# A vision tower on one core: from whole pairs over two drain turns to halves of a pair, one half-step apart

## The reference, cut to what matters

```python
q_feat = bilinear_sample(feature_map, ref)                    # 32 x 32 grid
h = gelu(layer_norm(q_feat @ W_o1 + b_o1, ln_g, ln_b))
sampled = bilinear_sample(feature_map, ref + off(h) * scale)  # 8 points for each token
out = softmax(q . k) @ v                                      # over the 8 points
...
h = concatenate([cls_tok, out])                               # 1025 tokens
x = layernorm(h); y = wkv(decay, first, x1 @ Wk, x1 @ Wv)     # recurrence over tokens
x = x + (sigmoid(x1 @ Wr) * y) @ Wo
x = x + sigmoid(h2 @ Wr_ffn) * (square(relu(h2 @ Wk_ffn)) @ Wv_ffn)
h = h + x;  h = h + relu(expert[argmax(router)](layernorm(h)))
```

## Time and profile before

| | |
|---|---|
| median of 3 runs | 2804.71 us (2804.19 to 2809.35) |
| profiled execution, its own time | 2803.6 us |
| its span (first to last instruction) | 2801.7 us |
| busy: PE, DVE, ACT, POOL | 2391.6, 2385.7, 1350.2, 1983.2 us |
| mean granted TensorE clock | 0.952 of full speed |
| transfers | 314.70 MB, of which 268.57 MB gathers |

### The profile page before, as it was taken

One profiled execution on the slowest core, in us unless ns is written; L12 is line 12 of the kernel. 1 busy time (PEld: TensorE's weight loads), 2 busy tenths in 40 slices (PEclk: granted clock), 3 DMA queues, 4 the chain that ended last, 5 costly groups with the idle time before them and its releaser, 6 DMA issues. The chain is left out here.

```text
span 2801.7 us, 34581 instructions
## 1 busy us (share of the span) xinstructions
PE 2391.6 (85%) x10646; PEld 1561.1 (56%) x10680; DVE 2385.7 (85%) x3808; ACT 1350.2 (48%) x2326; POOL 1983.2 (71%) x2052
## 2 busy tenths in 40 slices
PE   4588889888988888898888889888888988889887
PEld 4455555655655555655555556555556556555533
DVE  5889989889998989998898989888998988888741
ACT  2345444544544444464444446444444645444563
POOL 4777777777777777777777777777777777777400
PEclk7799999999999999999999999999999999999999
DMA  4333333434343343434334343433434343333200
GB/s 161 118 119 117 119 119 103 126 118 127 118 126 118 105 123 116 127 117 127 118 111 128 108 126 118 125 118 113 127 106 126 118 125 119 111 104 103 72 0 15
DMA packets 139228, 314.70 MB, mean 112 GB/s; under 512 B 68912, under 2 KB 69296, under 8 KB 134960
## 3 DMA queue, kind: packets, MB, share of 16 engines
q0 software_dynamic: 98304, 268.57, 32.7%
q1 hardware_dynamic: 40880, 45.58, 4.8%
HBM read 305.62 MB, written 8.40 MB: 112 GB/s over the span
## 5 line engine op out<-in xcount | busy, mean ns | idle before, releaser
L471 POOL DMA_INDIRECT gathered<-pixels,index x2048 | 1983.0, 968 | 649.2 <-issue 614.8
L527 PE MATMUL points_ps<-c_sb,weighed 128*128 128x128 f32 x4096 | 542.4, 290 | 230.8 <-DVE weighed L1063 230.3
L1063 DVE TENSOR_TENSOR weighed<-gathered,tables 128x1024 f32<-128x1024 f32 x512 | 600.4, 1214 | 125.8 <-DMA gathered<-pixels,index 123.9
L527 PEld LDWEIGHTS points_ps<-c_sb,weighed 128*128 128x128 f32 x4096 | 494.9, 150 | 339.7 <-DVE weighed L1063 286.4
L539 PE MATMUL kv_ps<-kv_sb,sampled_t 128*128 128x256 f32 x2048 | 473.4, 385 | 26.6 <-DVE products L1091 26.4
L721 ACT ACTIVATE sampled_t<-points_ps 128x512 f32<-128x512 f32 x256 | 153.1, 598 | 710.1 <-PE points_ps L527 710.1
L539 PEld LDWEIGHTS kv_ps<-kv_sb,sampled_t 128*128 128x128 f32 x2048 | 388.0, 192 | 112.6 <-DVE products L1091 41.2
L617 PE MATMUL work_ps<-nm,w_sb 128*128 128x512 f32 x544 | 291.6, 619 | 38.0 <-DVE xm L1253 35.3
L486 PE MATMUL work_ps<-hn,w_sb 128*128 128x512 f32 x544 | 267.4, 616 | 12.9 <-DVE hn L1115 10.2
L849 ACT ACTIVATE moe_hidden<-work_ps,v_sb 128x512 f32<-128x512 f32 x272 | 186.7, 687 | 161.5 <-PE work_ps L618 144.2
L1098 DVE TENSOR_REDUCE scores<-products 128x128 f32<-128x1024 f32 x128 | 246.0, 1922 | 0.0
(11 more groups left out here) (169 smaller groups left out, 3124.4 us busy)
## 6 DMA issues: line engine op xcount, KB each, us to landing
grid_px<-grid SPq DMA_DIRECT2D x32, 1024.0 KB, 5.6
gathered<-pixels,index POOLq DMA_INDIRECT x2048, 2.7
out<-rm SPq DMA_DIRECT2D x32, 256.0 KB
w_sb<-weights SPq DMA_DIRECT2D x1, 1984.0 KB, 8.9
moe_hidden<-consts SPq DMA_DIRECT2D x1, 512.0 KB, 9.8
attended<-cls SPq DMA_DIRECT2D x1, 512.0 KB, 11.5
c_sb<-consts SPq DMA_DIRECT2D x1, 192.0 KB, 5.2
w_sb<-weights SPq DMA_DIRECT2D x1, 192.0 KB, 5.1
```

Of the source, the lines that this page charges most:

```text
L471: pool.indirect_dma_start(gathered[:, n % RING, k * PATCH:(k + 1) * PATCH], None, pixels, bass.IndirectOffsetOnAxis(ap=index[:, n // TILES ...
L527: mm = pe.matmul(points_ps[:, j * P:(j + 1) * P], weighed[:, n % 2, at:at + 2 * C], ident, is_transpose=True, start=(q == 0), stop=(q == 3))
L1063: ins = dve.tensor_tensor(to[:, :, :, e, :], g[:, :, e, :, :], wt[:, :, e, :].unsqueeze(3).broadcast_to([P, HEADS // 2, 4, C]), ALU.mult)
```

## The change

The pipeline's unit becomes half a pair: 512 tokens of both images. A turn still samples one pair in 32 slots, but in its first 16 slots it samples the first half of both images and in its last 16 the second half. The mix and the experts run on halves, in parts: A is the first part of the mix ("early": `in` to `wo` and `add_mix`) on half 0 of the pair being sampled, in slots 20 to 31 of the same turn; B is the rest ("late": `cenf` to `dn`) of that half, in slots 0 to 4 of the next turn; C is both for half 1 (early in slots 4 to 15, late in 16 to 20); D and E are the experts for halves 0 and 1 (slots 5 to 15 and 21 to 31). One template of 16 slots is used for both half-steps, and the `LAST_` tables are gone. One turn without sampling follows turn 15 (turn 16: B, C, D and E). Turn 0 has only C and E for the class token, in half 1, and A.

Every stage that waited for two halves, and every ACT or DVE operation on 1024 tokens, becomes one on 512 that is done twice. The grid's load and the output's store, which SP issues, are split in the same way: each half-step loads 512 KB from each of two images and stores 128 KB to each of two. On SP the order in a turn was load, load, store; it is load, store, load, store, and a store waits for ACT's copy of `out` (slot 15 of its half-step).

```diff
-PIECES = 4
-PIECE = NQ // PIECES
+PIECES = 2
+PIECE = HALF // PIECES
...
-SCHEDULE = [
-    (0, 1, ["in0"]), (1, 2, ["cenm0", "cenm1"]), (2, 1, ["cena0"]), (2, 2, ["varm0", "varm1"]), (2, 1, ["vara0"]),
...
+TEMPLATE = [
+    (0, "late", ["cenf"]), (0, "late", ["varf"]), (1, "late", ["gate"]), (1, "late", ["up.0", "up.1"]),
+    (2, "late", ["up.2", "up.3"]), (3, "late", ["dn"]), (4, "query", ["qt0", "qt1"]), (4, "early", ["in"]),
...
+PART_OF = {"late": "BC", "early": "AC", "expert": "DE", "query": ("q0", "q1")}
+PART_SLOT = {"late": (0, 16), "early": (16, 0), "expert": (0, 16), "query": (0, 16)}
...
+EARLY_AT = {"mix_input": 6, "running_max": 8, "running_sums": 10, "mixed_sums": 12, "mixed_exponent": 13, "mixed": 14,
+            "add_mix": 15}
+LATE_AT = {"ffn_input": 1, "gate_exponent": 2, "add_ffn": 4}
+EXPERT_AT = {"moe_input": 6, "take_logits": 8, "choose": 9, "add_moe": 14}
...
             def iteration(it):
                 parts = parts_of(it)
-                for b in range(2):
+                for h in range(2):
                     if "q0" in parts:
-                        load_grid(it, b)
-                if 2 in parts:
-                    store(it)
+                        load_grid(it, h)
+                    if "DE"[h] in parts:
+                        store(it, "DE"[h])
...
-            def ffn_input(it):
-                for h in range(2):
-                    dve.wait_ge(stds_f.sem, stds_f.at(it, h + 1))
-                    dve.tensor_tensor(hn[:, cols(h)], xc[:, cols(h)], rs1[:, cols(h)],
-                                      ALU.mult).then_inc(ffn_in_ready.sem, 1)
...
+            def ffn_input(it, part):
+                run, h = run_of(it, part), half_of(part)
+                dve.wait_ge(stds_f.sem, stds_f.at(run, h))
+                dve.tensor_tensor(hn[:, cols(h)], xc[:, cols(h)], rs1[:, cols(h)], ALU.mult).then_inc(ffn_in_ready.sem, 1)
```

More of the change, by code:

```diff
@@ L57 @@
 T_GRID = 4 * TILES * HEADS
-T_DECAY = T_GRID + 4 * TILES
+T_DECAY = T_GRID + 2 * 4 * TILES
 SLOTS = 4 * (2 * TILES) // 2
-SCHEDULE = [
[11 rows of a table removed]
-]
[L80 to L86, removed]
@@ new lines, with schedule @@
+PART_OF = {"late": "BC", "early": "AC", "expert": "DE", "query": ("q0", "q1")}
+PART_SLOT = {"late": (0, 16), "early": (16, 0), "expert": (0, 16), "query": (0, 16)}
+def schedule():
+    rows = []
+    for half in range(2):
+        for slot, stage, names in TEMPLATE:
+            h = 1 - half if stage == "early" else half
+            rows.append((16 * half + slot, PART_OF[stage][h], names))
+    return rows
+SCHEDULE = schedule()
+QUERY_AT = {"grid_corners": 2, "features": 7, "normalised": 11, "gelu": 13, "sampling_points": 15}
@@ L97, with work_uses @@
 QUERIES_AT = (17, 1)
-LAST_SCHEDULE = [
[8 rows of a table removed]
[L108 to L116, removed]
 ROUND = float(2 ** 23)
 GELU_CUBE = 0.044715
-def work_uses(schedule, parts):
-    names = [(part, name) for _, part, group in schedule if part in parts for name in group]
+def work_uses(parts):
+    names = [(part, name) for _, part, group in SCHEDULE if part in parts for name in group]
     return {key: n for n, key in enumerate(names)}, len(names)
@@ L393, in all_iterations @@
                     steps.restart(eng)
-            for it in range(last_looped + 1, pairs + 2):
+            for it in range(last_looped + 1, pairs + 1):
                 turn(it)
@@ L415, in load_grid @@
                 sp.sem_inc(grid_requested.sem, 1)
[L416 to L433 removed]
+                of = slice(b * TILES // 2 * PATCH, (b + 1) * TILES // 2 * PATCH)
@@ new lines, in gate, with expert @@
+            def gate(run, h):
+                act.wait_ge(gate_exp_arg.sem, gate_exp_arg.at(run, h))
+                act.activation(rs2[:, cols(h)], rs2[:, cols(h)], ACT.Exp, scale=-1.0).then_inc(gate_ready.sem, 1)
+            def expert(it, part, names):
+                run, h, name = run_of(it, part), half_of(part), names[0]
+                if name == "cenm":
+                    act.wait_ge(written[h].sem, written[h].at(run - 1 + h, 0))
+                    centered(it, part, "cenm", xm, rm)
+                if name == "varm":
+                    inverse_stds(it, part, "varm", rm, stds_m.sem)
+                if name == "one":
+                    bank, done = full(act, it, part, "one")
+                    act.activation(choice_t[:, cols(h)], bank, ACT.Copy)
+                    act.activation(others_t[:, cols(h)], bank, ACT.Identity, bias=minus1_col).then_inc(done, 1)
+                if name.startswith("mu"):
+                    for use in names:
+                        k = int(use[-1])
+                        bank, done = full(act, it, part, use)
+                        at = V_MB1 + k % BLOCKS
+                        act.activation(moe_hidden[:, k, :], bank, ACT.Relu,
+                                       bias=v_sb[:, at:at + 1]).then_inc(done, 1)
+                if name == "out":
+                    bank, done = full(act, it, part, "out")
+                    act.activation(rm[:, cols(h)], bank, ACT.Copy).then_inc(done, 1)
@@ L1203, in gate_exponent, with add_mix @@
-            def gate_exponent(it):
-                dve.wait_ge(gate_log.sem, gate_log.at(it, 2))
-                for c in range(PIECES):
-                    last = dve.tensor_tensor(rs2[:, piece(c)], rs2[:, piece(c)], relu_r[:, piece(c)], ALU.add)
+                        step(dve.tensor_copy(state[:, 0:1], state[:, HALF + 1:HALF + 2]))
+            def add_mix(it, part):
+                h = half_of(part)
+                bank, done = full(dve, it, part, "wo")
+                dve.tensor_tensor(x1[:, cols(h)], x1[:, cols(h)], bank, ALU.add).then_inc(done, 1)
@@ L1305, in iteration @@
-                    if 2 in parts:
-                        if j == vector_at["moe_input"]:
-                            moe_input(it)
-                        if j == vector_at["take_logits"]:
-                            take_logits(it)
-                        if j == vector_at["choose"]:
-                            choose(it)
-                        for h in range(2):
-                            if j == vector_at[f"add_moe{h}"]:
-                                add_moe(it, h)
+                    for name, stage in (("ffn_input", ffn_input), ("gate_exponent", gate_exponent), ("add_ffn", add_ffn)):
+                        for part in parts_at(it, j, "late", LATE_AT[name]):
+                            stage(it, part)
@@ new lines, in iteration @@
+                    for name, stage in (("mix_input", mix_input), ("running_max", running_max),
+                                        ("running_sums", running_sums), ("mixed_sums", mixed_sums),
+                                        ("mixed_exponent", mixed_exponent), ("mixed", mixed), ("add_mix", add_mix)):
+                        for part in parts_at(it, j, "early", EARLY_AT[name]):
+                            stage(it, part)
+                    for name, stage in (("moe_input", moe_input), ("take_logits", take_logits), ("choose", choose),
+                                        ("add_moe", add_moe)):
+                        for part in parts_at(it, j, "expert", EXPERT_AT[name]):
+                            stage(it, part)
```

726 lines of the change are left out of this document (355 added, 371 removed), and 18 rows, old and new, of tables (LAST_SCHEDULE, SCHEDULE).

## The result

The changed kernel takes 3320.7 us (median of 4 runs, 3317.83 to 3322.5), the kernel before 2804.45 beside it: a ratio of 1.1836, interval 1.1815 to 1.1856. Forecast was 3341, with 3229 to 3477 for the likeliest case. The profiled run has a span of 3319.7 us and a mean granted clock of 0.903.

A forecast was written before the change was run, and what follows sets the result against it. POOL was taken to set the pace at 81.5 us a half-step, DVE next at 74.7. First half-step 120, 31 half-steps of 100.6 making 3118.6, drain 100.2: span 3338.8, so 3341 us, range 2980 to 3480.

The forecast's parts named there:

- the likeliest case: Whole kernel: half-steps of 97 to 105 us, 3229 to 3477 us in all, given 52%.
- What bounds the kernel: Sampling turns: POOL sets the pace at 81.5 us per half pair; DVE is occupied for 74.7, leaving 6.8 us for waits.
- What it adds: Operations done twice: 0.3 us of DVE start-up a half-step, 75 us of work; SP's grid load behind a store costs nothing.
- What it moves: Main term: dependent stages in the same or next slot make in-order DVE wait, 19.9 us a half-step.
- the walk: One half-step traced from DVE's slot 0: nine DVE waits, 19.9 us in sum, giving 94.9 us against POOL's 81.5.
- TensorE's clock: PE at 1.2 GHz after two long idle gaps: 2.85 us each, 5.7 us a half-step, making 100.6 us.
- The two long idles of the walk: PE idle from varm (38.6) to project (42.1), and from slot 8's sample (51) to slot 10's (60.6); 2.85 us lost behind each.
- the clock costs more: Rival: a third slow PE spell at the half-step's end and between cenf, varf and gate; 3601 us, above 3480 given 7%.
- The 4.7 us of turn 0: Rows of before: after 5.86 us idle, a sample took 3.67 for 1.97 and the project behind it 6.60 for 3.62.
- The sum: Whole kernel: first half-step 120 us, 31 of 100.6, drain 100.2, span 3338.8; 3341 us, 19% slower.
- half of 100.2 for each: Drain, new turn 16: each of two half-steps takes half of old turn 16's 100.2 us; 57 us saved, 111 possible.
- The signs: New profile: POOL often waits for weighed; hn, nm and others wait 2 to 4 us; clock 0.85 to 0.90; drain near 100.

The follow-up runs named there:

- lag3: Against lag: route, take_logits and choose a slot earlier, add_ffn a slot later, gate and up behind the exponentials; 2790.9 us, 0.9952 of the kernel before.
- sp_order: Against the changed kernel: SP's order back to load, load, store, store in a turn; 3325.08 us, 1.1842 of the kernel before.
- warm_full: Against the changed kernel: eleven unread PE products behind the sample of slots 8 and 24, filling PE's idle time; 3310.0 us, 1.1784 of the kernel before.
- late_first: Against the changed kernel: PE runs cenf and varf of slots 0 and 16 before that slot's sample, ACT their evictions before copy_points; 3208.26 us, 1.1434.
- lag: Against the changed kernel: experts a half-step later, mixed, wo and add_mix opening the next half-step, dependent stages two slots apart; 2848.81 us, 1.0153.
- late_tight: Against lag2: late stages as tight as in the changed kernel, wo, mixed and add_mix back in slots 14 and 15; 3084.15 us, 1.0995.
- lag2: Against lag: gate, up, gate_exponent, add_ffn, take_logits and choose a slot later, feature_std a slot earlier; 2890.68 us, 1.0298 of the kernel before.

## Why the prediction was right, and where not

- **What bounds the kernel** was right. POOL's 81.5 us is a floor and DVE's work with its room the second bound: across nine kernels the half-step is 75.2 to 76.0 us plus the waits, and in the three with waits under 6.5 us it is POOL's again. That working by halves costs nothing in a half-step, as long as POOL leads, is shown by lag3 (81.0 us).
- **What it adds**: SP's order costs nothing, as predicted (sp_order). The start-up of 0.3 us fits DVE's busy time (9 us more over 32 half-steps), but the changed kernel's DVE is occupied for 75.8 us of a half-step, not 75: 0.8 us, some 25 us of the whole, that the prediction didn't have.
- **What it moves**, the walk, named all nine waits. Its sum of 19.9 us was 3.6 short of the 23.5 of the half-step shown. Of this 1.5 lie at `ffn_input` and 1.4 at `gelu`, the two places that stand behind a `sample` at half clock; the others are within 0.5. That nine chains read from rows of before came out so close is the mechanism being right, and not luck.
- **TensorE's clock** is the term that was mis-sized: 5.7 us, where the waits of the half-step leave it those 3.6. The two long idles of the walk were the wrong picture. The `sample` of slot 10 was slow as said, but it cost 1.8 us, not 2.85; the `project` of slot 7 wasn't slow at all. Two other spells came instead, both behind idle times that only the rival "the clock costs more" had named: the `sample` of slot 0, and `gate`, `up.0` and `up.1`, 4.56 us in place of the 2.92 that `k`, `v` and `r`, of the same shape, take in the same half-step. All three are there in each of the 16 half-steps from 900 to 2500 us, 5.1 us of PE's time together. But DVE's `attend` behind `gate` waited only 0.2 us longer than in the walk, so the third spell hardly shows in the excess. From PE's timeline of the changed kernel:

```profile
1617.21 3.59 PE L533 MATMUL points_ps<-c_sb,weighed 128*128 128x128 f32 x16 [2.78 <-DVE weighed L1065]
...
1626.12 4.56 PE L492 MATMUL work_ps<-hn,w_sb 128*128 128x512 f32 x6 [2.17 <-DVE hn L1211]
...
1659.72 3.72 PE L545 MATMUL kv_ps<-kv_sb,sampled_t 128*128 128x256 f32 x16 [3.30 <-DVE products L1093]
...
1678.38 3.68 PE L533 MATMUL points_ps<-c_sb,weighed 128*128 128x128 f32 x16 [9.54 <-DVE weighed L1065]
```

  The 4.7 us of turn 0 took in a `project` behind the `sample`; here PE was at full speed again after each slow `sample`. The half clock explains up to 3.6 of 99 us, and 1.8 of them (`gelu`, in warm_full) are shown. The Trainium skill ("TensorE: Matmul & The Clock Gate", Part 1) puts the ramp under 1% of a typical kernel's span, in a passage on the first matmuls after a start. This kernel pays it anew in each half-step, so the measurement decides against that figure here, though by less than I had put.
- **The sum** was off in three terms that offset each other; that it came within 21 us of the result is in part luck. The first half-step took 128.7, not 120: POOL's first gather came at 28.41, not 26.06, the last `weigh` at 113.84, 3.6 us later than the sum has it, and `add_mix` waited 4.58 us for `wo`. The 31 half-steps took 98.9 each, not 100.6: 54 us less. The drain took 126.3, not 100.2, above even the 111: "half of 100.2 for each" was the wrong step, since a chain's latencies stay when its operations halve. The last `add_moe` waits 23.28 us for `mu` and `md` with nothing else to do. Part of the drain is the clock, which the sum left out there: 0.85 on average, against 0.95 in turn 16 of before, and `dn` took 5.37 us in place of 3.60 in both half-steps. How the 26 us divide between the two isn't shown.
- **The signs** came as listed, but for the clock (0.903 and not below 0.90), the drain, and `hn` and `nm`, which waited 5.1 and 4.3 us each time and not 2 to 4.

That the half clock lengthens a wait is shown for `gelu` (1.8 us, warm_full) and for `running_max` (1.7 us, late_first). For `ffn_input` it is only argued, since late_first changed the order there together with the clock. What makes one `project` slow and another not, behind the same idle time, stays open.

## What to carry to other kernels

When a pipeline is cut into finer steps, count for each in-order engine the time that it has left under the pace-setter's, and hold the sum of its waits against it; while the sum is smaller the cut is free in each step, and every us above it is paid in each step. In this kernel, stages that depend on each other through two engines wanted two slots between them, or a whole step between their parts: the lag of one half-step together with that spacing (lag, whose drain was longer) gave back nine tenths of the loss, and the lag with tight late stages (late_tight) less than half. A moved slot is checked on all lists, for it can take the cover of another wait, as lag2 did.

## What had not been expected of the hardware

TensorE's slow spells didn't follow the length of the idle time in front of them. `gate`, `up.0` and `up.1` were slow behind 2.17 us of idle (4.56 us in place of 2.92) and a `sample` behind 2.78 (3.59 in place of 1.91), but a `project` at 2.4 GHz behind 3.30 (3.72). Filling an idle stretch with 7.03 us of products left the `sample` behind the remaining 2.67 us at half clock (3.37 us); filling all of it cured that `sample` and slowed a `project` elsewhere (6.62 us), as did moving `cenf` and `varf` ahead of another `sample` (5.41 us). And a mean clock that rose from 0.903 to 0.938 bought nothing, because the work that raised it was work that nobody waited for.
